# A decoder layer with gated linear attention: output weights in float32r parts, and a reordered group of heads

## The reference

```python
q = _l2norm((x @ Wq).reshape(Bb, Tt, H, DK))      # H = 8, DK = DV = 128, x = layernorm(x)
k = _l2norm((x @ Wk).reshape(Bb, Tt, H, DK))
v = (x @ Wv).reshape(Bb, Tt, H, DV)
alpha = jax.nn.sigmoid(x @ Wg).reshape(Bb, Tt, H, DK)
def step(S, qkva):
    S = a_t[..., None] * S + k_t[..., None] * v_t[:, :, None, :]
    o_t = jnp.einsum('bhkv,bhk->bhv', S, q_t)
    return (S, o_t)
...
x = x + o.reshape(Bb, Tt, H * DV) @ Wo
x = x + softmax(layernorm(x) @ (ctx @ W.T).T) @ ctx
x = x + experts(layernorm(x))                      # two of eight, gelu, weighted
```

## Time and profile before

| what | value |
|---|---|
| three runs, median (lowest to highest) | 496.46 us (495.48 to 499.6) |
| the profiled execution, its own time | 497.58 us |
| its span in the profile | 495.8 us |
| PE busy (share of the span) | 469.4 us (95%) |
| DVE busy | 361.5 us (73%) |
| ACT busy | 337.2 us (68%) |
| POOL busy | 108.0 us (22%) |
| mean granted clock of PE | 0.979 |

### The profile page before, as it was taken

One profiled execution on the slowest core, in us unless ns is written; L12 is line 12 of the kernel. 1 busy time (PEld: TensorE's weight loads), 2 busy tenths in 40 slices (PEclk: granted clock), 3 DMA queues, 4 the chain that ended last, 5 costly groups with the idle time before them and its releaser, 6 DMA issues. The chain is left out here.

```text
span 495.8 us, 23878 instructions
## 1 busy us (share of the span) xinstructions
PE 469.4 (95%) x10228; PEld 389.0 (78%) x10228; DVE 361.5 (73%) x1038; ACT 337.2 (68%) x797; POOL 108.0 (22%) x102
## 2 busy tenths in 40 slices
PE   1799999999999999999999999999999999999786
PEld 1588788877888788878888788878888888877675
DVE  5777887655679788784769788885759588884463
ACT  4858777766668867777577877777767877765421
POOL 1022222211221222242022222242122222231031
PEclk9989999999999999999999999999999999999778
DMA  8900000001001010022001010013010010011023
GB/s 326 332 3 5 3 5 3 4 3 45 5 3 46 3 46 3 3 62 73 22 25 46 5 46 3 4 46 87 3 46 5 3 46 3 5 46 44 1 64 107
DMA packets 15273, 20.15 MB, mean 41 GB/s; under 512 B 1217, under 2 KB 12993, under 8 KB 15169
## 3 DMA queue, kind: packets, MB, share of 16 engines
q1 hardware_dynamic: 13888, 14.43, 9.1%
q0 software_dynamic: 1280, 4.20, 2.9%
HBM read 16.53 MB, written 2.10 MB: 38 GB/s over the span
## 5 line engine op out<-in xcount | busy, mean ns | idle before, releaser
L482 ACT COPY states<-states 128x512 f32<-128x512 f32 x128 | 80.8, 631 | 47.9 <-DVE states L706 32.7
L392 POOL TENSOR_TENSOR rnorm<-norm_sq,neg_half 128x4 f32<-128x4 f32 x32 | 45.1, 1409 | 265.6 <-DVE norm_sq L769 265.6
L706 DVE TENSOR_TENSOR states<-states,spans 128x512 f32<-128x512 f32 x96 | 66.4, 692 | 8.1 <-ACT states L482 0.9
L1190 PEld LDWEIGHTS lo_bank<-states 128*32 128x32 f32 x5120 | 51.0, 110 | 22.9 <-issue 19.1
L1279 PE MATMUL acc<-wo_sb,oT_sb 128*128 128x256 f32 x256 | 60.8, 380 | 0.9 <-ACT oT_sb L509 0.9
L1190 PE MATMUL lo_bank<-states 128*32 128x16 f32 (+1 forms) x5120 | 57.8, 188 | 0.0
L757 DVE COPY_PREDICATED blocks<-owned,lo_bank 128x64 f32<-128x64 uint32 (+1 forms) x160 | 41.0, 256 | 22.2 <-PE lo_bank L1190 17.5
L1179 PE MATMUL ring<-wv_sb,xnT 128*128 128x256 f32 x384 | 55.7, 295 | 1.2 <-DVE wv_sb L962 1.2
L1166 PE MATMUL ring<-xnT,wk_sb 128*128 128x512 f32 x192 | 53.7, 416 | 2.2 <-DVE xnT L825 1.7
L1166 PE MATMUL ring<-xnT,wq_sb 128*128 128x512 f32 x192 | 53.5, 413 | 0.0
L1166 PE MATMUL ring<-xnT,wg_sb 128*128 128x512 f32 x192 | 51.0, 401 | 0.5 <-DVE wg_sb L962 0.2
(11 more groups left out here) (181 smaller groups left out, 784.5 us busy)
## 6 DMA issues: line engine op xcount, KB each, us to landing
x_buf<-x_dram SPq DMA_DIRECT2D x4, 512.0 KB, 4.3
ctxT_sb<-ctxT_dram SPq DMA_DIRECT2D x8, 256.0 KB, 3.8
ctx_sb<-ctx_dram SPq DMA_DIRECT2D x4, 512.0 KB, 3.8
out_dram<-x_mid SPq DMA_DIRECT2D x6, 256.0 KB
states<-wk_dram SPq DMA_DIRECT2D x1, 1024.0 KB, 5.6
states<-wg_dram SPq DMA_DIRECT2D x1, 1024.0 KB, 7.8
states<-wq_dram SPq DMA_DIRECT2D x1, 1024.0 KB, 9.8
v_sb<-wv_dram SPq DMA_DIRECT2D x1, 1024.0 KB, 11.9
```

The lines of the kernel that those rows point to most:

```text
L392: nc.gpsimd.tensor_tensor(rnorm[:, m % 4, GB:2 * GB], norm_sq[:, GB:2 * GB], neg_half[:, GB:2 * GB], ALU.pow).then_inc(rk_set, 1)
L482: nc.scalar.copy(halves(l, 2 ** (l - 1), False), halves(l - 1, 2 ** (l - 1), False)).then_inc(carry_set, 1)
L706: nc.vector.tensor_tensor(halves(l, w, True), halves(l - 1, w, True), by, ALU.mult).then_inc(decayed, 1)
L1190: last = mm(lo_bank[BLOCK * r:BLOCK * r + BLOCK, to:to + columns], view(states, left + start, [[1, BLOCK]]), view(states, right + start, q ...
```

## The change

Three things are changed, and what they need around them.

- **Wo in float32r parts.** wo_sb gets an upper and a lower part. Wo is loaded in four pieces of two heads into x_mid and rowsT, which are free then; ACT rounds one piece to the upper part and DVE subtracts it to get the lower one, at the end of heads 0, 2, 4 and 6. oT_sb holds the upper part (ACT) and the lower part (DVE, new `oT_lower`, placed behind the q decay of the next head) in place of two buffers. The output projection makes twelve products: eight with oT's upper part, then it waits for the lower part and makes four. Four semaphores are new.
- **The tail.** The transposes x2T move from part "A" of head 2 to part "B", behind the output projection. The exponentials of the scores move on ACT from "early" to "mid" of head 3: behind the sigmoid of the next head and the copies `expand_blocks`.
- **o_scaled** of the heads with n mod 8 = 2, 3, 4 moves ahead of decays 2 to 4.
- **ctx and ctxT share one tile**, for space. ctx is loaded when the keys' products are done, ctxT of the next group when the cross products are done.

```diff
-        wo_sb = sb("wo_sb", [P, H, D])
+        wo_sb = sb("wo_sb", [P, 2, H, D], F32R)
-        ctx_sb = sb("ctx_sb", [P, GB, D])
         ctxT_sb = sb("ctxT_sb", [P, KC, GB, T])
+        ctx_sb = ctxT_sb[:].rearrange("p c b t -> p (c b t)").rearrange("p (b d) -> p b d", b=GB)
-        oT_sb = sb("oT_sb", [P, 2, N])
+        oT_sb = sb("oT_sb", [P, 2, N], F32R)
+        stage_o = tuple(tile[:, 2 * D * k:2 * D * k + 2 * D] for tile in (
+            x_mid[:].rearrange("p b d -> p (b d)"), rowsT[:].rearrange("p c n -> p (c n)")) for k in range(2))
...
-            if place == "A" and h == 2 and t >= 0:
+            if place == "B" and h == 2 and t >= 0:
                 found = [("x2T", t, 0), ("x2T", t, 1)]
...
-                        "o": (o_set, n + 1), "oT": (oT_set, n + 1)}[kind]
+                        "o": (o_set, n + 1), "oT": (oT_lo, n + 1)}[kind]
...
+        def wo_read_by(n):
+            i, h = divmod(n, H)
+            return (wo_mm, 2 * i + 2) if h == H - 1 else (wo_read, (H - 1) * i + h + 1)
...
-            sp.dma_start(wo_sb[:], wo.rearrange("(h p) n -> p h n", p=P)).then_inc(w_in, 16)
+            for j, heads in enumerate(stage_o):
+                sp.dma_start(heads.rearrange("p (h n) -> p h n", h=2),
+                             wo[2 * P * j:2 * P * j + 2 * P].rearrange("(h p) n -> p h n", p=P)).then_inc(wo_in, 16)
...
             load_ctxT(0)
-            load_ctx(0)
             for i in range(1, NG):
                 sp.wait_ge(tail_mm, TAIL["keys", i - 1, 1])
-                load_ctxT(i)
+                load_ctx(i - 1)
...
                 sp.wait_ge(tail_mm, TAIL["cross", i - 1, 1])
-                load_ctx(i)
+                load_ctxT(i)
+            sp.wait_ge(tail_mm, TAIL["keys", NG - 1, 1])
+            load_ctx(NG - 1)
...
             def oT_out(n):
                 act.wait_ge(oT_mm, n + 1)
-                nc.scalar.copy(oT_sb[:, n % 2], ring_of(("oT", n))[:]).then_inc(oT_set, 1)
+                if n > 0:
+                    act.wait_ge(*wo_read_by(n - 1))
+                nc.scalar.copy(oT_sb[:, HI], ring_of(("oT", n))[:]).then_inc(oT_set, 1)
...
-                    if at == (3, "early"):
+                    if at == (3, "mid"):
                         probs_out(t)
...
+            def split_wo(j):
+                act.wait_ge(wo_in, 16 * WO_PAIRS)
+                nc.scalar.copy(wo_sb[:, HI, 2 * j:2 * j + 2].rearrange("p h d -> p (h d)"), stage_o[j]).then_inc(wo_hi, 1)
...
+                if n < H and n % 2 == 0:
+                    split_wo(n // 2)
...
+            def oT_lower(n):
+                dve.wait_ge(oT_set, n + 1)
+                nc.vector.tensor_tensor(oT_sb[:, LO], ring_of(("oT", n))[:], oT_sb[:, HI].bitcast(F32),
+                                        ALU.subtract).then_inc(oT_lo, 1)
+            def split_wo(j):
+                dve.wait_ge(wo_hi, j + 1)
...
                     q_decayed(n + 1)
+                if n >= 2:
+                    oT_lower(n - 2)
                 tail_part(n, "late")
                 for k in range(KEEPS):
                     keep(n, k)
+                if n % H in (2, 3, 4):
+                    o_scaled(n - 1)
...
-                if n >= 1:
+                if n >= 1 and n % H not in (2, 3, 4):
                     o_scaled(n - 1)
...
                 tail_part(n, "end")
+                if n < H and n % 2 == 0:
+                    split_wo(n // 2)
+            oT_lower(U - 2)
             weigh_up(NG - 2)
             o_scaled(U - 1)
+            oT_lower(U - 1)
...
                 pe.wait_ge(oT_set, n + 1)
+                if i == 0 and h % 2 == 0:
+                    pe.wait_ge(wo_split, h // 2 + 1)
...
-                for b in range(GB):
-                    z, m = b // 2, b % 2
-                    last = mm(accs[z][:, D * m:D * m + D], oT_sb[:, n % 2, T * b:T * b + T], wo_sb[:, h],
-                              start=(h == 0 and m == 0), stop=(h == H - 1 and m == 1))
-                    if h == H - 1 and m == 1:
-                        last.then_inc(wo_mm if i < NG - 1 else half_mm[z], 1)
+                for part, (a, w) in enumerate(PARTS):
+                    if a == LO:
+                        pe.wait_ge(oT_lo, n + 1)
+                    for b in range(GB):
+                        z, m = b // 2, b % 2
+                        last = mm(accs[z][:, D * m:D * m + D], oT_sb[:, a, T * b:T * b + T], wo_sb[:, w, h],
+                                  start=(h == 0 and m == 0 and part == 0), stop=(h == H - 1 and m == 1 and part == 2))
+                        if h == H - 1 and m == 1 and part == 2:
+                            last.then_inc(wo_mm if i < NG - 1 else half_mm[z], 1)
+                if h < H - 1:
+                    last.then_inc(wo_read, 1)
```

More of the change, by code:

```diff
@@ L134, in decoder_kernel @@
         stage_v = v_sb[:].rearrange("p r b h v -> p (r b h v)")
+        WO_PAIRS = H // 2
+        stage_o = tuple(tile[:, 2 * D * k:2 * D * k + 2 * D] for tile in (
+            x_mid[:].rearrange("p b d -> p (b d)"), rowsT[:].rearrange("p c n -> p (c n)")) for k in range(2))
         staged = ((wk_sb, stage_k), (wg_sb, stage_g), (wq_sb, stage_q), (wv_sb, stage_v))
@@ L145, in decoder_kernel @@
         wk_in, wg_in, wq_in, wv_in = (sem(n) for n in ("wk_in", "wg_in", "wq_in", "wv_in"))
+        wo_in = sem("wo_in")
         w_in, c_in, ctx_in, ctxT_in, out_free = (
@@ L158, in decoder_kernel @@
             sem(n) for n in ("decayed", "span_set", "kept", "norm_sq_set", "v_set", "o_set"))
+        oT_lo, wo_hi, wo_split, wo_read = (sem(n) for n in ("oT_lo", "wo_hi", "wo_split", "wo_read"))
         rk_set, rq_set, ln_stat, ln_var, ln_rstd, ln_out = (
@@ L309, in span_at @@
             return 2 * (N // 4 - N // 2 ** l)
-        N_W, N_C = 16 * 4, 16 * 2
+        N_W, N_C = 16 * 3, 16 * 2
         block = stack.enter_context(nc.Block())
@@ L327, in load_ctx @@
             def load_ctx(i):
-                sp.dma_start(ctx_sb[:], ctx[GB * i:GB * i + GB].rearrange("b t d -> t b d")).then_inc(ctx_in, 16)
+                sp.dma_start(ctx_sb, ctx[GB * i:GB * i + GB].rearrange("b t d -> t b d")).then_inc(ctx_in, 16)
             def store(t, z):
@@ L788, in o_scaled @@
                                         ALU.mult).then_inc(o_set, 1)
+            def oT_lower(n):
[4 more added lines that the diff above has]
+                dve.wait_ge(wo_hi, j + 1)
+                upper = wo_sb[:, HI, 2 * j:2 * j + 2].bitcast(F32).rearrange("p h d -> p (h d)")
+                nc.vector.tensor_tensor(wo_sb[:, LO, 2 * j:2 * j + 2].rearrange("p h d -> p (h d)"), stage_o[j], upper,
+                                        ALU.subtract).then_inc(wo_split, 1)
             def residual(t):
```

## The result

The changed kernel takes 502.4 us in the median of four runs (500.2 to 504.8) and 502.1 in six later ones; the kernel before takes 497.3 and 497.3 beside them. The ratios are 1.012 (95% interval 1.008 to 1.017) and 1.012 (1.008 to 1.016): slower by over 1%. 502 was predicted. Executions over 1.5% above the fastest of their kernel are left out of medians and averages (four of 93 of the kernel before, one of twelve of the kernel with the scaling back). The profiled execution took 500.2 with a span of 498.3. From the page: the busy time of PE and VectorE, the granted clock in 40 slices, and the group of Wo's products.

A forecast was written before the change was run, and what follows sets the result against it. PE (TensorE) was taken to set the pace. Terms -8.5 + 0.9 + 7.1 - 1.6 + 2.7 + 0.5 + 0.8 = +1.9 gave 498.4 us; +3.6 for the clock made 502, range 494 to 506.

The forecast's parts named there:

- stall and clock falls: Fourth heads of three groups: PE waits 2.3 to 2.4 us for exponentials and the clock falls; 502 us, chance 0.55.
- Wo block: Output projection: twelve float32r products save 0.28 us a head, 9.0 in all; the last projection instead +0.2.
- Lower part of oT in third heads: PE waits 0.3 us at Wo for VectorE's added subtraction, three groups: +0.9 us.
- Exponentials: Fourth heads: gate projection to transposes of o takes 6.15 us, PE stands 2.3 to 2.4 longer; +7.1 us.
- the reload off the path: Products with attnT no longer wait for the sigmoid table's reload: 0.65, 0.7 and 0.3 us, together -1.6.
- k projection of the sixth heads: It waits about 1.0 us for v scaling, delayed by early o_scaled and the subtraction; three groups: +2.7 us.
- End: Heads 30 and 31: VectorE runs back to back; the subtraction and its wait add time: +0.8 us.
- Clock: The 2.4 us PE waits lower the clock in most of three groups, 1.2 us each: +3.6 us.
- Rival 1: The stall comes but the clock stays up: 498.4 us; chance 0.25.
- Rival 2: Exponentials are not last to arrive at the transposes of o: 491.3 us, or 488.6 without VectorE's waits; chance 0.12.
- Rival 3: A table switch amid work costs up to twice its 1.28 us row: 506 us; chance 0.05.
- Rival 4: The float32r Wo block gets no cheaper, waiting for its lower part in most heads: 507 us; chance 0.03.

The follow-up runs named there:

- the kernel with the scaling back: Changed kernel with o_scaled put back behind the decays in all heads: 501.0 us, ratio to before 1.009.
- the subtraction cut: Changed kernel with the subtraction for oT's lower part over 32 of 512 columns, except in the first head: 499.0 us, ratio to before 1.003.
- the three pairs: o_scaled early against behind the decays: changed kernel 502.1 and 501.0 us; exponentials early 498.8 and 496.5; exponentials between sigmoid and attnT copies 497.7 and 494.8.
- exponentials between: Changed kernel with the four exponentials between the sigmoid and the four copies into attnT: 497.7 us, ratio to before 1.003.
- both with the short subtraction: Changed kernel with exponentials early and o_scaled behind the decays, subtraction for oT's lower part over 32 of 512 columns: 493.4 us, ratio to before 0.993.

## Why the prediction was right, and where it was not

The time, 502.0, is within 0.4 of both medians, and the likeliest case, stall and clock falls, is what came. That it is so near is luck in part, as the last lines say. Point by point, with the profiled pair's 5.5 us at the last projection's start taken apart by the distances of PE's blocks in the two traces:

- **Wo block**: predicted -0.28 each, -8.7 in all. Measured -0.27, and the float32 block ahead of it 0.08 shorter. This second part was not in the sum; it makes some -10 us. After the waits of the next two points, -8.0 are left for both blocks.
- **Lower part of oT in third heads**: predicted 0.3 each, measured 0.4. In the fifth heads it was costed at nothing, but there the normalized cross rows stand behind it on VectorE and PE's transposes of them start 0.3 late. The prediction took them for ordinary heads with cover and had not looked. With the subtraction cut both waits go.
- **Exponentials**: the chain of 6.15 came as 6.17, the three waits as +7.2 (7.1 predicted), the reload off the path as -1.6 (-1.6). These terms are the surest. What failed is reading them as the price of the edit: undoing it gave 3.3 us, not 5.5 plus clock, and some 2.2 of the 3.3 are clock, since beside the other edits smaller waits hide under the long one.
- **k projection of the sixth heads**: predicted 0.9 each, measured 0.8 by the distance of the blocks' starts, +2.3 in all. The chain was named rightly. With the scaling back the wait is gone, with the subtraction cut it is 0.44 after 0.54: most of it is the early scaling's. What the prediction did not ask is what the early scaling gives: against a wait of 0.4 at the gate projection that it avoids, it costs 1 to 3 us by the three pairs. A like delay of the k projection comes in heads 2 and 4 of the first group, 0.4 each, where one place and 0.5 had been predicted.
- **End**: predicted +0.8, measured about +1.0: the transposes of o in head 30 wait 0.97 for VectorE's scaling.
- **Clock**: predicted 1.2 for each group, 3.6. Over five profiled executions with 2.3 us waits the clock fell behind 8 of 15 such waits (1, 3, 1, 1 and 2 of three); two heads with a fall take 31.36 instead of 30.08, so 1.3 each, and 8/15 x 3 x 1.3 = 2.1 us. The runs say the same: the four kernels with that wait have a mean clock of 0.977 to 0.979, all nine without it 0.981 to 0.984; 0.005 at 0.41 per 0.001 is 2.0 us. "In most" should have been "in half". Rival 1 is a matter of each execution: with one fall in three it took 500.2.
- **Not foreseen**: in this execution PE stood 1.27 us in the middle of the scores' block in head 18, waiting for nothing that the profile shows.

So -8.0, +7.2, -1.6, +3.1 (k projections, heads 2 and 4), +1.0, clock +1.3 and the stop 1.3 make 4.3, and the remaining 1.2 is not assigned to single places; it may lie in the start and small distances. The prediction's total was right in part by luck, because its errors cancel: Wo's gain 1.5 us too small, the clock 1.5 us too dear, the fifth heads' 1 us left out, the unexplained stop.

Rival 2 (exponentials not last) is refuted by the three waits. Rival 3, the dearer table switch, is too: 279.65 + 1.28 leads to 280.95 with no more time between. The Trainium skill (ScalarE: Activation LUTs, What ACT_TABLE_LOAD costs) puts a drain on top of each load; the trace shows none. Rival 4 is refuted by the 1.56 us block.

## What to carry to other kernels

A wait on the bounding engine is not the price of the edit that makes it: before you add it to a sum, ask which other engine would be late at the next blocks if it were gone, since PE then only waits there. A cheaper product form that needs one more pass on VectorE gains only where the other engines have time free in that stretch, not on average: here cheaper blocks worth some 10 us, bought with 0.6 us a head on an engine with a quarter of its time free, left the kernel as fast as before (497.0 us). About a third of the loss hung on the length of that pass (3.1 us back with a short one); the rest stayed, for the most part in the fourth and fifth heads of the groups, where PE then waits for ScalarE and VectorE. Where an activation table has to be switched inside a chain, place it directly behind the one activation that somebody waits for, ahead of copies that nobody needs yet.

## What the hardware showed beyond this

- **The clock and the length of a wait.** Behind waits of 2.3 us in the middle of full work the granted clock fell 8 times in 15, each time to a mean of 0.57 to 0.67 over the 4 us behind the wait, a mix of the 1.2 GHz level and the full one. Behind waits of 1.2 us it fell in none of 12, in four kernels. The Trainium skill (TensorE: Matmul & The Clock Gate, The HAM clock gate) would let it fall only behind longer idle gaps than these; the 8 falls disagree. Why one wait of the same length and place has it and another has not, no run here tells.
- **A float32r block overlaps the float32 one ahead of it** by 0.08 us more than a float32 block does: 0.91 us from the start of the products with attnT to that of Wo's in head 21, against 0.99 in head 16 before.
- **A stop without a cause in the profile.** In four of the profiled executions (changed kernel, exponentials between, both with the short subtraction) PE stood 1.3 to 1.5 us behind the ninth of the sixteen products of the scores in head 18, in the others not at all or for 0.3. In the changed kernel, in a window around it, the queue of instructions had one transfer of 0.02 MB; but the kernel with early exponentials alone has such a transfer there too, and no stop. That PE waits for its program is only a guess; it stays open.

```profile
271.59 1.27 PE L1343 MATMUL ring<-projT,rowsT 128*128 128x128 f32 x9
274.13 0.94 PE L1343 MATMUL ring<-projT,rowsT 128*128 128x128 f32 x7 [1.27 <-issue]
```
